# Two expert layers with the output halves in the inner loop, so that consecutive products go to two PSUM banks in turn

## The reference, cut to what matters

```python
h = jnp.einsum('bfd,edh->bfeh', x, W1) + b1          # first layer, 256 -> 256, 8 experts
h = jax.nn.relu(_bn(h, g1, be1, m1, v1))
h = jnp.einsum('bfeh,ehk->bfek', h, W2) + b2          # second layer, 256 -> 256
h = jax.nn.relu(_bn(h, g2, be2, m2, v2))
y = jnp.einsum('bfeh,ehd->bfed', h, Wo) + bo          # third layer, 256 -> 256
return jnp.einsum('bfed,fe->bfd', y, w)               # w = softmax(feat @ Wr + br)
```

## Time and profile before

| what | value |
|---|---|
| time, median of 3 | 1018.16 us (1016.85 to 1018.79) |
| span of the profiled execution, first to last instruction | 1012.8 us |
| mean granted TensorE clock | 0.952 of full speed |
| TensorE busy | 911.4 us, 90% of the span, 4984 matmuls and 4984 weight loads |
| VectorE, ScalarE, GpSimd busy | 799.5 us, 589.4 us, 377.3 us |

### The profile page before, as it was taken

One profiled execution on the slowest core, in us unless ns is written; L12 is line 12 of the kernel. 1 busy time (PEld: TensorE's weight loads), 2 busy tenths in 40 slices (PEclk: granted clock), 3 DMA queues, 4 the chain that ended last, 5 costly groups with the idle time before them and its releaser, 6 DMA issues.

```text
span 1012.8 us, 14669 instructions
## 1 busy us (share of the span) xinstructions
PE 911.4 (90%) x4984; PEld 790.1 (78%) x4984; DVE 799.5 (79%) x1517; ACT 589.4 (58%) x1206; POOL 377.3 (37%) x408
## 2 busy tenths in 40 slices
PE   6897899989888999898746689999999999999997
PEld 5686788878777778777535578999988889898986
DVE  6778799988888888988786788775565778786867
ACT  4730456655656556666254566667665767666663
POOL 0167777777777777777773000000000000000000
PEclk9988899999999999998868799999999999999999
DMA  8434454454444444445563002000000010100013
GB/s 260 151 91 138 141 140 129 134 141 141 125 139 139 123 140 138 128 138 140 165 194 100 6 17 63 29 2 32 1 9 24 1 32 1 32 1 1 1 37 91
DMA packets 50362, 89.00 MB, mean 88 GB/s; under 512 B 9733, under 2 KB 33337, under 8 KB 50268
## 3 DMA queue, kind: packets, MB, share of 16 engines
q0 software_dynamic: 18768, 52.88, 19.0%
q1 hardware_dynamic: 30780, 34.66, 11.2%
q10 hardware_dynamic: 719, 0.27, 0.1%
HBM read 81.10 MB, written 6.68 MB: 87 GB/s over the span
## 4 chain that ended last, share of the span: by engine, by line
PE 41%; POOL 34%; issue 13%; DVE 7%; ACT 3%; DMA 2%; SPq 0%; POOLq 0%; DVEq 0%; ACTq 0%
POOL G L491 34%; PE bank L1043 9%; PE bank L1045 9%; PE bank L1044 9%; PE bank L1107 2%; PE bank L1110 2%; PE bank L837 2%; DMA x_in<-in_x 1%; PE bank L1108 1%; PE bank L1109 1%; PE bank L916 1%; ACT hid L741 1%; PE bank L872 1%; ACT sums L718 1%; PE bank L830 1%
## 5 line engine op out<-in xcount | busy, mean ns | idle before, releaser
L491 POOL DMA_INDIRECT G<-projected_rows,src_l x391 | 374.5, 958 | 166.6 <-issue 118.3
L741 ACT ACTIVATE hid<-bank,faff 128x512 f32<-128x512 f32 (+2 forms) x224 | 157.7, 723 | 111.1 <-PE bank L1045 109.3
L916 PE MATMUL bank<-G,oh 128*128 128x264 f32 x782 | 188.6, 400 | 21.3 <-DVE G L1422 21.1
L916 PEld LDWEIGHTS bank<-G,oh 128*128 128x128 f32 x782 | 153.5, 198 | 49.9 <-DVE G L1422 22.7
L1422 DVE TENSOR_TENSOR G<-G,bank 128x3072 f32<-128x3072 f32 (+1 forms) x33 | 109.1, 3306 | 0.0
L1716 DVE TENSOR_TENSOR hil<-hid,hil 128x1024 fp32r<-128x1024 f32 (+2 forms) x56 | 60.8, 1086 | 48.3 <-ACT hil L749 48.3
L1043 PE MATMUL bank<-frh,ew 128*128 128x512 f32 (+3 forms) x228 | 84.3, 370 | 4.4 <-DVE frl L1691 4.4
L1044 PE MATMUL bank<-frl,ew 128*128 128x512 f32 (+3 forms) x228 | 82.8, 363 | 0.0
L1045 PE MATMUL bank<-frh,ew 128*128 128x512 f32 (+3 forms) x228 | 82.8, 363 | 0.0
L1043 PE MATMUL bank<-hil,ew 128*128 128x512 f32 (+2 forms) x224 | 81.6, 364 | 0.0
L1045 PE MATMUL bank<-hil,ew 128*128 128x512 f32 (+2 forms) x224 | 81.2, 362 | 0.0
(11 more groups left out here) (344 smaller groups left out, 2059.3 us busy)
## 6 DMA issues: line engine op xcount, KB each, us to landing
dstb<-targets SPq DMA_DIRECT2D x32, 384.0 KB, 3.7
G<-projected_rows,src_l POOLq DMA_INDIRECT x391, 2.8
projected_rows<-sums SPq DMA_DIRECT2D x25, 132.0 KB, 2.2
x_in<-in_x SPq DMA_DIRECT2D x3, 1024.0 KB, 9.6
out<-feat_rows SPq DMA_DIRECT2D x23, 128.0 KB, 2.2
U<-in_x SPq DMA_DIRECT2D x4, 512.0 KB, 6.0
TT<-in_W SPq DMA_DIRECT2D x8, 256.0 KB, 3.3
wqkv<-in_W SPq DMA_DIRECT2D x8, 256.0 KB, 3.9
```

Of the source, the lines that this page charges most:

```text
L491: g.indirect_dma_start(out=G[slot][:, c, :], out_offset=None, in_=table[:, :], in_offset=bass.IndirectOffsetOnAxis(ap=src_l[:, grp, c:c + ...
L741: A.activation(hid[layer][:, m, 0:cols], bank[2 * layer + m][:, 0:cols], ACT.Relu, bias=faff[:, 2 * layer + 1, j:j + 1], scale=faff[:, 2 * ...
L916: ins = T.matmul(b_seg[g % 2][:, 0:ROW], oh[g % 2][:, c, :], G[g % SLOTS][:, c, :], start=(c == 0), stop=(c == ch - 1))
```

## The change

In both of the first two layers of every expert, the loop over the output half m is moved inside. Before, all six products of half 0 were issued, then the six of half 1. Now each term (input half k, which part of the weights, which part of the data) is issued for half 0 and at once for half 1, so that consecutive products write banks 0, 1, 0, 1, ... (banks 2, 3, 2, 3, ... in the second layer). The order of the terms within one half is as before, and so are the number of products, their shapes, the weight loads and the waits ahead of each layer. Both signals of a layer are now raised by its last two products. The third layer is as it was.

```diff
--- before.py
+++ after.py
@@ -1044,6 +1044,15 @@
                 T.matmul(out_, lh, rl, start=False, stop=False)
                 return T.matmul(out_, ll, rh, start=False, stop=(k == KC - 1))
 
+            def split_products(outs, w, x):
+
+                terms = [(k, wi, xi) for k in range(KC) for wi, xi in ((0, 0), (0, 1), (1, 0))]
+                last = []
+                for i, (k, wi, xi) in enumerate(terms):
+                    last = [T.matmul(out_, w[:, wi, k, m * P:(m + 1) * P], x[xi][:, k], start=(i == 0), stop=(i == len(terms) - 1))
+                            for m, out_ in enumerate(outs)]
+                return last
+
             def weights(e, m):
                 pe.wait_ge(s["w_hi"], 3 * e + m + 1)
                 pe.wait_ge(s["w_lo"], 3 * e + m + 1)
@@ -1060,12 +1069,9 @@
                     if e == 0:
                         pe.wait_ge(s["frl_ready"], -(-(start + hi) // P))
                     nodes_ = slice(start + lo, start + hi)
-                    for m in range(KC):
-                        w = slice(m * P, (m + 1) * P)
-                        for k in range(KC):
-                            ins = split_product(bank[m][:, lo:hi], ew[:, par, 0, 0, k, w], ew[:, par, 1, 0, k, w],
-                                                FRH[:, k, nodes_], FRL[:, k, nodes_], k)
-                        if hi == cols:
+                    last = split_products([bank[m][:, lo:hi] for m in range(KC)], ew[:, par, :, 0], [FRH[:, :, nodes_], FRL[:, :, nodes_]])
+                    if hi == cols:
+                        for ins in last:
                             ins.then_inc(s["h1_mm"], 1)
 
             def second(n):
@@ -1076,11 +1082,9 @@
                 pe.wait_ge(s["h1_hi"], n + 1)
                 pe.wait_ge(s["h1_lo"], n + 1)
                 need(pe, s["h2_r"], n * KC)
-                for m in range(KC):
-                    w = slice(m * P, (m + 1) * P)
-                    for k in range(KC):
-                        ins = split_product(bank[2 + m][:, 0:cols], ew[:, e % 2, 0, 1, k, w], ew[:, e % 2, 1, 1, k, w],
-                                            hidh[0][par][:, k, 0:cols], hidl[0][par][:, k, 0:cols], k)
+                last = split_products([bank[2 + m][:, 0:cols] for m in range(KC)], ew[:, e % 2, :, 1],
+                                      [hidh[0][par][:, :, 0:cols], hidl[0][par][:, :, 0:cols]])
+                for ins in last:
                     ins.then_inc(s["h2_mm"], 1)
 
             def third(n):
```

## The result

The changed kernel took 1019.26 us, the median of 20 runs (1017.57 to 1021.17), against 1016.74 us for the kernel before, also 20 runs (1014.37 to 1019.53). The ratio is 1.0023, with a 95% interval of 1.0014 to 1.0031: slower by 2.3 us. The forecast had been 1.0 us slower. The forecast time of 1019.2 us looks closer than it was, because the kernel before came out 1.4 us lower in 20 runs than in the first three; that the two times meet is luck.

The account below looks back on a forecast made before the run. TensorE's own rate was taken to bound most of the changed stretch, with ScalarE's delay counting at both ends. Rate 0, step 0 +0.6 and end +0.4 us made +1.0 us on 1018.16, so 1019.2 us; range 1016.2 to 1022.6 us.

Parts of the forecast that it names:

- Part 1, the rate: TensorE's distance between product starts: unchanged by alternating banks, zero cost, with 2.3 us either way for the range.
- The first rival: Neighbouring products in one bank cost time, so alternating gains up to 12 us, about 1007 us in all; chance 0.17.
- Part 2, the later half: Half 0 is ready later for ScalarE and VectorE: nothing in steady steps, +0.6 us at step 0, +0.4 us at the end.
- The steady steps: From 684 to 1000 us, 43 steps: a delay of 0.5 us each stays hidden behind TensorE's work, costing nothing.
- The end: From step 54's second layer to VectorE's last add: ScalarE's later pair costs +0.4 us, bounds 0 and 0.7.
- Step 0: First step, nothing running ahead: ScalarE's later pair delays the chain up to step 4 by +0.6 us, bounds 0 and 0.8.
- the prediction's own sign: The prediction is wrong if the delay of step 0 vanishes on the way to step 4's first layer at 603.87 us.
- The prediction's bound of 0: Lower bound at step 0: no loss if a gap in the chain, longest 1.11 us at 584.33 us, takes the delay up.
- The second rival, the clock: TensorE's clock falls to 0.5 at the wait before step 4: two stretches cost 3.4 us, 1022.6 us; chance 0.10.
- Nothing makes the wait longer: Argument against the clock falling: TensorE's wait before step 4 keeps its 2.90 us and only lies 0.6 us later.
- the bounds of the two ends: Largest losses allowed for the later half: 0.8 us at step 0 and 0.7 us at the kernel's end.
- the room left for a change of rate: Allowance in the range of 2 ns for each of 1130 products with a new kind of neighbour, 2.3 us up or down.

Follow-up runs that it names:

- e0: The changed kernel run once more, with nothing altered; ratio 1.0025 to the kernel before.
- e2: The changed kernel with the old loop order given back in the first layer of step 0 and both layers of the last two steps; ratio 1.0010 to the kernel before.
- e5: The kernel before with 16 extra products of 128 columns in TensorE's wait before the experts; ratio 0.9996 to the kernel before.
- e6: The kernel before with one extra ScalarE copy in step 0's first layer, no loop turned; ratio 1.0002 to the kernel before.
- e3: The changed kernel with ten extra products of 512 columns in TensorE's wait before step 4; ratio 1.0000 to the kernel before.
- f1: The kernel before with ten extra products in the wait before step 4, run beside three other filled kernels on one chip; ratio 0.9981, mean 1015.66 us.
- e4: The kernel before with ten extra products of 512 columns in TensorE's wait before step 4; 1014.89 us, ratio 0.9971 to the kernel before.
- e1: The kernel before with the loops turned only in the first layer of step 0; ratio 1.0015 to the kernel before.

## Why the prediction was right, and where it was not

**Part 1, the rate: right.** I took zero from the distances at the changes of bank that were there already, and zero it is: 2.73 us for twelve products before and after, 107.4 us from step 4 to the gates in both orders, and -0.09 us (plus or minus 0.5) for the turned middle. The first rival, that neighbours in one bank pay for it, is out.

**Part 2, the later half: right in place, and the size at step 0 holds only in some executions.** The steady steps cover it, as worked out: no wait on TensorE appears. The end was put at +0.4 us and measured at 0.39. Step 0 was put at +0.6 us; between the first two profiles it was 0.56, with the same chain behind it up to step 4. In e0 it was nothing, and by the prediction's own sign (the delay of step 0 vanishes on the way to step 4) that part was wrong for such an execution. What I had not seen is that the trace was of an execution in which the clock came up late. Where it comes up early, VectorE reaches the subtraction from its own work without waiting, and the delay is hidden. The line for this was in VectorE's timeline of the kernel before:

```profile
573.18 0.17 DVE L1678 TENSOR_SCALAR nodes<-mv 128x4 f32<-128x4 f32 x1
573.69 1.22 DVE L1716 TENSOR_TENSOR hil<-hid,hil 128x1024 fp32r<-128x1024 f32 x1 [0.34 <-ACT hil L749]
```

The wait ahead of the subtraction is only 0.34 us long. If TensorE's step 0 is over earlier by more than that, VectorE's own work is the later one. The prediction's bound of 0 looked for a gap further down the chain, at 584.33 us, and not here.

**The second rival, the clock: given a chance of 0.10, and there in the first profile.** Its place was right, its price of 1.7 us for each stretch near (1.5 for one, 2.8 for two), and its chance was not. I had reasoned that the kernel before kept its clock through that wait, and had one execution to say so. Of the seven profiles with that wait left open, six have the fall; of the seven with it filled, none. (Six in seven is no rate for all executions: two of the six, e2 and e5, are of slow ones.) A fall costs 1.5 us (108.9 less 107.4) or 2.8 us (110.2 less 107.4). It isn't the change's alone: e2, e5 and e6 have it with the old order in the first layer of step 0, and filling the wait wins 2.2 us with the turned loops (e0 to e3) and 1.9 and 2.4 us with the old ones (f1 and e4 against the kernel before that ran beside each). The step of the prediction that failed is the argument against this rival. "Nothing makes the wait longer" is true, the wait was 2.90 us again; but it took the full clock behind that wait, seen in one trace, for a property of the kernel.

**The sum.** Forecast +1.0 us, measured +2.3 us (1.4 to 3.2). On the 1018.16 us that the sum starts from, a loss of 2.3 us would be 1020.5 us. That is inside the range, but more than the bounds of the two ends allow together (0.8 + 0.7 = 1.5 us): it fits by the room left for a change of rate, which didn't come, and for the fall of the clock, given a chance of 0.10. With the clock held, the ends cost 0.96 us (plus or minus 0.5), which is the sum that was forecast; the profiles give 0.4 us where the clock comes up early in step 0 and 0.9 us where it comes up late, so that the agreement is partly luck.

What stays open is the rest, 2.3 - 0.96 = about 1.3 us, with an uncertainty of 1 us, which shows only where the wait is left open. It may not be there at all: e3 and e4, each against the kernel before that ran beside it, lie 2.4 us apart (plus or minus 1.2) with the wait filled, which would leave nothing over. If it is there, the turned kernel could meet the fall more often. A later wait does not make it longer in these profiles. Where the clock came up early in step 0 (e0, e1, e2, e5) TensorE reached the wait 49.3 us from the first cut and the clock was down for 6.8 us; where it came up late and the first layer was turned or ScalarE delayed (the changed kernel, e6) at 50.3 and 50.4 us, and it was down for 3.4 us; in the kernel before at 49.7 us, and it held. With one profile of each kernel none of this is shown to be the rule.

**A version that beats both** is the old order with the ten extra products before step 4: 0.9971 (0.9956 to 0.9986) and, run again as f1, 0.9981 (0.9971 to 0.9990) of the kernel before.

## What to carry to other kernels

Before an inner loop is turned, look at the distance of starts where the pattern that the change makes already occurs: the trace held the answer on the banks. Then ask who was working on the half that used to be ready first; the cost shows only where that engine's result is on the path, at the beginning and at the end of a pipeline. And where the matrix engine waits for some microseconds ahead of a dense stretch, look at the granted clock behind the wait in more than one execution: throwaway products inside the wait can be worth more than the order of the real ones.

## What the runs showed of the hardware that was not expected

- Around a wait of 2.9 us on TensorE, with the engine busy on both sides, its clock went from 2.4 to 1.2 GHz in six of seven profiles: for 3.4 us, beginning 1.1 and 1.4 us behind the wait, or for 6.8 us, beginning in the last microsecond of the wait. With ten products of 512 columns in that wait, it did not, in seven of seven. The Trainium skill (TensorE: Matmul & The Clock Gate, HAM oscillation — how this bites in real kernels) describes such falls between stretches of work, but for longer idle gaps than this one; the measurement decides.
- The same code ahead of the experts took between 550.95 and 553.40 us in 14 profiles on several chips, and executions of the kernel before spread over 8 us (1014.2 to 1022.8). A term of half a microsecond is seen in the cuts of a profile and not in a median.
- Products of 512 columns in this rounded float format start 227 ns apart, and of 384 columns 173 ns, in one bank or in two.
